# Three exchanges in the first microseconds: parameter rows before the input's loads, the context's normalisation before the input's statistics, the second half of the keys before the input's transposition

## What is computed

```python
xq = layer_norm(x, qn_w, qn_b)              # x: 2 x 2048 x 512
ctx = layer_norm(context, cn_w, cn_b)       # context: 2 x 77 x 512
q = (xq @ q_w).reshape(B, N, H, D)
kv = (ctx @ kv_w).reshape(B, M, 2, H, D)
k, v = kv[:, :, 0], kv[:, :, 1]
attn = jnp.einsum('bnhd,bmhd->bhnm', q, k) * scale
attn = softmax(jnp.where(xa_mask, neg, attn))
out = jnp.einsum('bhnm,bmhd->bnhd', attn, v).reshape(B, N, C) @ proj_w + proj_b
x = x + out
h = layer_norm(x, n2_w, n2_b)
return x + gelu(h @ fc1_w + fc1_b) @ fc2_w + fc2_b
```

## Time and profile before

| | us |
|---|---|
| median of 3 runs | 1047.71 |
| lowest, highest | 1047.18, 1049.47 |
| the profiled execution | 1051.2 |
| its span, first to last instruction | 1049.3 |
| PE busy | 1033.1 (98% of the span) |
| DVE busy | 822.3 (78%) |
| ACT busy | 434.5 (41%) |
| POOL busy | 359.2 (34%) |

### The profile page before, as it was taken

One profiled execution on the slowest core, in us unless ns is written; L12 is line 12 of the kernel. 1 busy time (PEld: TensorE's weight loads), 2 busy tenths in 40 slices (PEclk: granted clock), 3 DMA queues, 4 the chain that ended last, 5 costly groups with the idle time before them and its releaser, 6 DMA issues.

```text
span 1049.3 us, 16369 instructions
## 1 busy us (share of the span) xinstructions
PE 1033.1 (98%) x5857; PEld 857.7 (82%) x5857; DVE 822.3 (78%) x1323; ACT 434.5 (41%) x766; POOL 359.2 (34%) x259
## 2 busy tenths in 40 slices
PE   8999999999999999999999999999999999999998
PEld 6788888888888777888778888878888888888887
DVE  7899999999997898887877676676766677666655
ACT  4344344444444566445533343342433352232221
POOL 3466566667787673233404000303100310300000
PEclk9999999999999999999999999999999999999999
DMA  7012122122210277564557535345536343834312
GB/s 267 8 47 71 51 92 74 63 62 83 81 42 22 74 297 233 188 232 160 197 213 258 225 131 191 124 159 174 227 131 234 118 164 126 312 120 172 124 67 81
DMA packets 52800, 149.33 MB, mean 142 GB/s; under 512 B 11313, under 2 KB 19545, under 8 KB 44531
## 3 DMA queue, kind: packets, MB, share of 16 engines
q1 hardware_dynamic: 52139, 147.25, 39.3%
q10 hardware_dynamic: 584, 1.06, 0.3%
HBM read 108.13 MB, written 39.85 MB: 141 GB/s over the span
## 4 chain that ended last, share of the span: by engine, by line
PE 93%; DVE 4%; issue 1%; DMA 0%; ACT 0%; POOL 0%; SPq 0%; DVEq 0%; ACTq 0%
PE bank L1801 32%; PE bank L1771 28%; PE bank L1604 8%; PE bank L1648 8%; PE bank L1585 5%; PE bank L1636 4%; PE bank L1617 3%; PE bank L1780 1%; PE bank L1595 1%; PE bank L1567 1%; PE bank L1625 1%; DVE acc L1409 1%; DVE hop L1371 1%; DVE gT L1401 1%; DVE w1r L1366 1%
## 5 line engine op out<-in xcount | busy, mean ns | idle before, releaser
L1801 PE MATMUL bank<-w2r,gT 128*128 128x512 f32 x1536 | 359.7, 391 | 2.2 <-DVE acc L1409 2.0
L1801 PEld LDWEIGHTS bank<-w2r,gT 128*128 128x128 f32 x1536 | 286.7, 188 | 64.2 <-DVE acc L1409 5.1
L1771 PE MATMUL bank<-hop,w1r 128*128 128x512 f32 x1344 | 314.2, 392 | 4.0 <-DVE hop L1371 3.0
L1771 PEld LDWEIGHTS bank<-hop,w1r 128*128 128x128 f32 x1344 | 252.3, 189 | 58.2 <-issue 4.9
L1409 DVE TENSOR_TENSOR acc<-bank,acc 128x512 f32<-128x512 f32 x256 | 176.7, 691 | 103.8 <-PE bank L1801 97.9
L1396 DVE TENSOR_TENSOR ybuf<-bank,ybuf 128x512 f32<-128x512 f32 x224 | 148.6, 688 | 82.3 <-PE bank L1771 74.2
L1046 ACT ACTIVATE ybuf<-ybuf,cols 128x512 f32<-128x512 f32 x128 | 91.6, 716 | 155.5 <-DVE ybuf L1396 155.5
L684 POOL TENSOR_TENSOR S<-S,rsum 128x1232 f32<-128x1232 f32 x32 | 75.3, 2354 | 61.6 <-DVE rsum L1202 61.6
L1401 DVE TENSOR_TENSOR gT<-ybuf,gT 128x512 fp32r<-128x512 f32 x128 | 92.9, 747 | 0.0
L649 POOL TENSOR_TENSOR hrs<-hve,mhalf 128x1 f32<-128x1 f32 x32 | 18.0, 562 | 213.6 <-DVE hve L1381 213.6
L792 POOL TENSOR_TENSOR acc<-acc,fc2b 128x512 f32<-128x512 f32 x32 | 44.0, 1391 | 134.7 <-DMA acc<-x_scratch 134.6
(11 more groups left out here) (111 smaller groups left out, 1450.8 us busy)
## 6 DMA issues: line engine op xcount, KB each, us to landing
w1r<-w_scratch SPq DMA_DIRECT2D x24, 1792.0 KB, 7.3
w2r<-w_scratch SPq DMA_DIRECT2D x24, 1024.0 KB, 5.4
w_scratch<-w1r SPq DMA_DIRECT2D x8, 1792.0 KB, 6.2
xr<-in_x SPq DMA_DIRECT2D x32, 256.0 KB, 2.9
x_scratch<-xr SPq DMA_DIRECT2D x32, 256.0 KB, 2.0
hring<-x_scratch SPq DMA_DIRECT2D x32, 256.0 KB, 3.0
acc<-x_scratch SPq DMA_DIRECT2D x32, 256.0 KB, 4.0
w_scratch<-w2r SPq DMA_DIRECT2D x8, 1024.0 KB, 4.9
```

Source lines behind the costliest of these rows:

```text
L1771: mm = pe.matmul(bank_[:, :], w1r[:, w1_slot(s), c, w, kk * P:(kk + 1) * P], hop[i][:, d, kk, :], start=(kk == 0 and n == 0), stop=(kk == ...
L1801: mm = pe.matmul(bY[t % 2][:, :], gT[s % 2][:, j, d, t * P:(t + 1) * P], w2r[:, s % 2, j, w, :], start=(n == 0), stop=(n == 5))
```

## The change

On SP the three parameter rows are issued ahead of the input's first two tiles. On DVE the context is normalised ahead of the statistics of the input's tile 0. On PE `keys(1)` stands ahead of `x_T(0)` and `x_T(1)`. ACT and POOL have the same instructions in the same order as before.

```diff
         sp.dma_start(cx[0:M, :, :], ctx.rearrange("b m c -> m b c")).then_inc(d_ctx, 16)
+        for i in range(3):
+            load_row(sp, i)
         for t in range(UT):
             load_x(static(0), t)
-        for i in range(3):
-            load_row(sp, i)
...
                 columns()
+                ctx_normed()
                 stats((0,))
-                ctx_normed()
                 stats((1,))
...
                 ctx_T()
                 q_bias(0)
                 keys(0)
+                keys(1)
                 x_T(0)
                 x_T(1)
-                keys(1)
                 for c in range(1, KT):
                     q_bias(c)
```

## The result

| | median us | lowest to highest | runs |
|---|---|---|---|
| before | 1046.87 | 1046.09 to 1050.21 | 11 |
| changed kernel | 1052.19 | 1049.69 to 1057.93 | 11 |

The changed kernel takes 1.0057 times as long (95% interval 1.0044 to 1.007): 5.3 us slower by the medians, outside the range that was predicted. Its runs also lie further apart than those of before. Timed again beside other runs of before, the same kernel gave 1.0047 (1.0031 to 1.0064).

The account below looks back on a forecast made before the run. DVE was taken to bound the start from 17.54 us, PE the body. Rows -1.5 + 0.25, keys(1) +2.15 and faster keys(0) -0.2 made +0.7 us, giving 1048.4 us (before: 1047.71), range 1046.6 to 1050.2.

Parts of the forecast that it names:

- What bounds the start: Start of the kernel: DVE bounds it from 17.54 us, so the body moves by as much as x_T(0).
- The price of keys(1) in front: PE's start: sixteen passes of keys(1) now stand ahead of x_T(0), +2.15 us.
- Rows earlier: Start, up to keys(0): rows land at 6.15 instead of 7.9; -1.5 us, with 0.25 taken back.
- the loss by later landings: Loads behind the rows: the input's later issue delays what lands later, between nothing and 0.7 us, taken as 0.25.
- The clock over the keys: PE in keys(0): the upper clock comes sooner, between -0.33 and 0 us, taken as -0.2.
- The bound that was named: keys(0) on PE: up to all of it at half rate if the wait for q_w delays the clock, +2.1 us.
- rival 3: Start: full 0.7 us of DMA shift and all of keys(0) at half rate; +3.2 us, 1050.9; chance 0.04.
- Rival 2: Next unit's x_T(0): PE pauses 2.1 us, lower clock follows, 1.7 us on the body; 1050.1; chance 0.09.
- slower by over 0.2%: Whole kernel: chance 0.13, from rivals 2 and 3, half of rival 4 and a little of the sum's upper end.

Follow-up runs that it names:

- rows_alone: The kernel before with only the parameter rows issued ahead of the input's loads; ratio to before 1.0012.
- input_first: The kernel before with rows and context moved ahead as in the change, but both halves of the keys behind the input's transposition; 1.0004 of before.
- after_wide_both: The changed kernel with both long pauses of PE filled by six wide warming matmuls in all; 1.0015 of before.
- before_again: The kernel before, unchanged, run again for a second trace; ratio 0.9993.
- after_again: The changed kernel, unchanged, run again for a second trace; 1.0047 of before.
- keys_alone: The kernel before with only keys(1) moved ahead of the input's transposition; 1.0044 of before.
- after_fill_first: The changed kernel with PE's first pause filled: 10 warming matmuls ahead of the first q_bias and 3 behind it; 1.004 of before.
- after_query_weights_ahead: The changed kernel with the load of q_w tile 0 issued right behind the parameter rows, ahead of the input's tiles; 1.0042 of before.
- context_and_keys: The kernel before with the context normalised earlier and keys(1) moved ahead, the loads in the old order; 1.0025 of before.
- after_wide_second: The changed kernel with only PE's second pause filled, by three wide warming matmuls; 1.0032 of before.

## Why the prediction was wrong, point by point

**What bounds the start: right.** From the start of `x_lo` to the start of the body it is 13.95 us in both traces of before (17.54 to 31.49, 16.23 to 30.18), in the changed kernel (20.41 to 34.36), and in rows_alone (18.91 to 32.86). DVE's thirteen microseconds are rigid, and `x_T(0)` is the lever, until, as in input_first, PE itself becomes late.

**The price of keys(1) in front: right in kind and size.** +2.15 was booked, and after_wide_both, which has little else left, stands 1.6 us behind before over all runs and 2.4 between runs at full clock.

**Rows earlier: this step failed, in three terms.** First, the rows landed before 5.39 and not at 6.15; that was worth nothing, and only made PE's wait longer. Second, the loss by later landings was put at 0.25 us, from a range of 0 to 0.7; tile 0 of `q_w` landed 0.96 us later than in the earlier trace rows (and 1.7 later than in the second trace of before, where it took 6.2 us; in the second trace of the changed kernel, though, it landed at 10.35), so that `keys(0)` started at 13.25 and not at 12.7. Third, the start to set it against was not 13.96: that was one execution's, with the lower rate under `q_bias`; the second trace has 12.79. The whole term, booked at -1.25, is +0.46 between 13.25 and 12.79; from one pair of traces to another it lies between that and -1.48 (12.48 less 13.96), so it is no dependable gain.

**The clock over the keys: wrong sign, and the step that failed with the most weight.** The sum booked -0.2 for a PE that gets up to speed sooner. It did get up sooner, and fell back behind a pause that the prediction put at nothing: it had `ctx_T` end at 10.4, past the landing of `q_w` at 10.16. With the rows at 5.39, and the twelve passes of warming at 1.92 us where 2.86 was booked, `ctx_T` ended at 8.7, and PE waited 2.49 us. The keys took 6.07 instead of 4.3, +1.8. The bound that was named (up to +2.1) holds; it was given as rival 3 a chance of 0.04.

**Rival 2 was the mechanism, and was given 0.09.** PE's second pause was forecast at 2.1 us and measured at 2.13 and 2.15; the lower clock followed in both traces of the changed kernel. Its price was less than the 1.7 booked, since part of that stretch fell into PE's second wait. Between the start of the body and the end of the `values` behind it,'s order of work takes 4.91 us in before_again (30.18 to 35.09) and 6.17 in the changed kernel (34.36 to 40.53): +1.26.

Together, against the second trace of before: keys later 0.46, keys(1) and the clock over both 3.73 (6.07 less 2.34), so `x_T(0)` 4.18 later, and 1.26 behind it: 5.4 us, where the medians differ by 5.3. That the two agree so well is in part luck. These two executions themselves differ by only 3.8 us in span (1050.2 and 1046.4). The first of the MLP's matmuls of L1771 starts 5.3 us later (362.3 and 357.0), the last of them 3.8 (1024.8 and 1021.0): on the way before_again stood still for 2.38 us near 700 us, and the first trace of the changed kernel did not. Against after_again, which has that pause too, the account closes: the body 3.96 later, 1.52 behind it, and 1.62 more for the 42 passes after the pause near 700, part of them at the lower clock (11.42 and 9.80), less 0.15 for the shorter pause, make 6.95; the spans differ by 7.0 (1053.4 and 1046.4). The mistake behind the numbers is that the pauses were kept out of the sum, and that rivals 2 and 3 were treated as exclusive, each on top of it. Both come from PE standing still ahead of its operands, and both came, in one execution.

**The range** reached to rival 2 (1050.1), not to rival 3 (1050.9), and not to both, and the chance of slower by over 0.2%, 0.13, was far too low.

## What to carry to other kernels

Work out where the engine with the clock will stand still before asking what it will finish sooner: an edit that lets PE begin earlier, with its operands no earlier, only lengthens a pause, and a pause of some 2 us was mostly paid twice here, in waiting and in the rate behind it. When an early step is brought forward, ask for each of its successors what else it waits for; the second and third gates stood within a microsecond of the first. And take two traces of the kernel before a sum over its first microseconds: they differed by 1.3 us with nothing changed.

## What the runs showed of the hardware that was not expected

The lower clock behind a pause is a matter of the single execution. At the change of blocks PE stood still for 2.29 us in one trace of before and the clock was 0.52 behind it; in the second trace of the same kernel it stood still for 2.38 us at the same place and the clock stayed up (PE's instruction, and the stretch behind it with the clock third from the end):

```profile
701.34 3.00 PE L1771 MATMUL bank<-hop,w1r 128*128 128x512 f32 x12 [2.38 <-DVE hop L1371]
...
703.00:707.00 4.00, 4.00 (x19) 3.30 (x19) 1.83 (x2) 0.60 (x1) 0.00 (x0) 1.00 0.40 146
```

The second pause of the changed order of keys was 2.13 to 2.15 us long in six traces; behind it the clock was at 0.50 in five (both of the changed kernel, keys_alone, after_fill_first, after_query_weights_ahead) and stayed at 1.00 in the sixth (context_and_keys). Shorter ones count as well: behind a first pause of 1.66 us in after_wide_second the clock was 0.50 from 13 to 16 us, and the 32 passes of the keys took 6.11. What decides between the two outcomes no run here shows.

In after_again the clock was at the lower level three times (over the first `q_bias` and most of the keys, behind the second pause, behind the pause near 700 us), and this profiled run took 1055.23 us against a lowest of 1050.13. That fits the wide scatter of the changed kernel: it has two more places where this can happen. The row of the granted clock can print full speed in the first microseconds although matmuls there take twice as long: in rows_alone it reads 1.00 throughout, while sixteen passes of the keys take 4.32 us, up to 17.81. There the rate has to be read from durations.

With twenty-six small matmuls near 10 and 30 us, PE waited 6.5 us near 700 us for nothing that a semaphore shows; with six large ones that fill the same time the longer of the two waits, 4.52 us, was absent. Why is not shown.
